# Two fused attention blocks in float32: the low part of phi on the two halves of the TensorE rows

## What is computed

```python
# layer 0, per image: x is [128, 1024]
theta = W_theta @ x + b_theta            # [64, 1024]
phi   = W_phi   @ x + b_phi              # [64, 1024]
f     = softmax(theta.T @ phi / sqrt(64))   # [1024, 1024], over the keys
x     = x + W_fuse @ (x @ f.T) + b_fuse
# layer 1
h = group_norm(x, 32 groups) * gn_w + gn_b
q, k, v = q_w @ h + q_b, k_w @ h + k_b, v_w @ h + v_b    # [128, 1024] each
f = softmax(q.T @ k / sqrt(128))
x = x + p_w @ (v @ f.T) + p_b
```

## Time and profile before

| | |
|---|---|
| Median of three runs | 2052.92 us |
| Span of the profiled execution | 2050.9 us (its own device time isn't given; the median lies 2.0 us above the span) |
| TensorE busy | 2024.2 us, 99% |
| VectorE busy | 1635.8 us, 80% |
| ScalarE busy | 1504.8 us, 73% |
| GpSimd busy | 1301.5 us, 63% |
| Mean granted TensorE clock | 0.999 of 2.4 GHz |

### The profile page before, as it was taken

The page is one execution under the profiler, slowest core; times in us unless marked ns, Lnnn a source line. Parts: engine busy times, 40 slices in busy tenths (PEclk is TensorE's granted clock), DMA queues, the critical chain, the costliest instruction groups (busy, mean ns, idle before and its releaser), DMA issues.

```text
span 2050.9 us, 39045 instructions
## 1 busy us (share of the span) xinstructions
PE 2024.2 (99%) x11460; PEld 1724.3 (84%) x11460; DVE 1635.8 (80%) x2538; ACT 1504.8 (73%) x2696; POOL 1301.5 (63%) x1669
## 2 busy tenths in 40 slices
PE   7899999999999999999999999999999999999998
PEld 5788888888888888888888888888888888888886
DVE  6788788878888887888888887888888888878875
ACT  5777777777777777777777777777777777777764
POOL 4666656666666666666665666666666656666654
PEclk9999999999999999999999999999999999999999
DMA  2111111111111011111111111111111111111100
GB/s 62 52 36 48 41 41 41 36 46 41 41 51 37 34 41 51 41 41 36 46 41 41 43 36 44 41 51 41 41 36 46 41 41 41 36 46 41 36 16 31
DMA packets 38326, 84.71 MB, mean 41 GB/s; under 512 B 4640, under 2 KB 5536, under 8 KB 38304
## 3 DMA queue, kind: packets, MB, share of 16 engines
q1 hardware_dynamic: 38304, 84.43, 13.2%
HBM read 34.08 MB, written 16.78 MB: 25 GB/s over the span
## 4 chain that ended last, share of the span: by engine, by line
PE 96%; DVE 0%; POOL 0%; issue 0%; ACT 0%; ACTq 0%; POOLq 0%
PE o_ps L317 35%; PE s_ps L317 28%; PE t_ps L331 21%; PE m_ps L317 6%; PE m_ps L425 3%; PE m_ps L427 1%; PE m_ps L409 0%; PE m_ps L405 0%; DVE et_lo L595 0%; DVE neg_max L605 0%; DVE y_sb L628 0%; ACT e L537 0%; POOL h_lo L718 0%; ACT et_hi L476 0%; POOL e L702 0%
## 5 line engine op out<-in xcount | busy, mean ns | idle before, releaser
L702 POOL TENSOR_SCALAR e<-e,rden 128x1024 f32<-128x1024 f32 x512 | 578.2, 1129 | 548.4 <-DVE rden L585 544.9
L476 ACT ACTIVATE et_hi<-t_ps 128x512 fp32r<-128x512 f32 x1024 | 557.5, 597 | 456.5 <-PE t_ps L331 455.3
L595 DVE TENSOR_TENSOR et_lo<-t_ps,et_hi 128x512 fp32r<-128x512 f32 x1024 | 659.9, 684 | 240.8 <-ACT et_hi L476 231.2
L605 DVE TENSOR_REDUCE neg_max<-s_ps 128x1 f32<-128x1024 f32 x512 | 622.0, 1215 | 2.2 <-PE s_ps L317 2.2
L537 ACT ACTIVATE e<-s_ps,neg_max 128x1024 f32<-128x1024 f32 x512 | 574.8, 1123 | 9.0 <-DVE neg_max L605 4.0
L331 PEld LDWEIGHTS t_ps<-ident_sb,e 128*128 128x128 f32 x4096 | 477.2, 140 | 75.0 <-POOL e L702 8.9
L331 PE MATMUL t_ps<-ident_sb,e 128*128 128x128 f32 x4096 | 531.7, 273 | 6.3 <-POOL e L702 5.5
L317 PE MATMUL o_ps<-et_hi,v_hi 128*128 128x512 f32 x1024 | 421.5, 412 | 2.1 <-DVE y_sb L628 1.9
L317 PE MATMUL o_ps<-et_lo,v_hi 128*128 128x512 f32 x1024 | 402.6, 393 | 0.0
L317 PE MATMUL o_ps<-et_hi,v_lo 128*128 128x512 f32 x1024 | 399.9, 391 | 0.0
L317 PE MATMUL s_ps<-phi,theta 128*128 128x512 f32 x1024 | 301.8, 417 | 1.3 <-ACT e L537 1.0
(11 more groups left out here) (95 smaller groups left out, 2193.1 us busy)
## 6 DMA issues: line engine op xcount, KB each, us to landing
xs<-in_x SPq DMA_DIRECT2D x32, 512.0 KB, 3.4
phi<-phi SPq DMA_DIRECT2D x64, 256.0 KB, 3.1
xr<-in_x SPq DMA_DIRECT2D x32, 512.0 KB, 3.3
x_res<-x SPq DMA_DIRECT2D x64, 256.0 KB, 2.3
out_y<-y_sb SPq DMA_DIRECT2D x64, 256.0 KB, 2.1
w_f<-in_w_fuse_t SPq DMA_DIRECT2D x1, 64.0 KB, 2.4
ident_sb<-in_ident SPq DMA_DIRECT2D x1, 64.0 KB, 2.1
p_t<-in_p_w_t SPq DMA_DIRECT2D x1, 64.0 KB, 2.2
```

What stands on the lines that cost most here:

```text
L476: nc.scalar.activation(et_hi[t // GROUP % 2][:, GROUP * half:GROUP * (half + 1), cols], t_ps[half][:, :].rearrange("k (b q) -> k b q", b=G ...
L595: nc.vector.tensor_tensor(et_lo[g][:, blocks, cols], t_ps[half][:, :].rearrange("k (b q) -> k b q", b=GROUP), et_hi[g][:, blocks, cols].bi ...
L605: nc.vector.tensor_reduce(neg_max[:, s % 4:s % 4 + 1], s_ps[:, s % 2, :], AX.X, ALU.max, negate=True).then_inc(s_max, 1)
L702: return nc.gpsimd.tensor_scalar(*args)
```

## The change

In layer 0 the products with phi's low part no longer take theta's low part along. Each uses 64 rows: the one for the first half of the keys takes theta's high part and phi's low part in rows 0:D, the one for the second half takes them in rows D:C. For this, theta's high part is needed in rows 64 to 127 as well, in a new buffer `theta_low`, which a further DMA fills behind the one of L303. So the term theta low x phi low is left out of the sum. The two full products come first, then the pair, which writes to the two different PSUM banks of the slot's scores.

```diff
+        theta_low = sb("theta_low", [C, N], F32R)
...
                     sp.wait_ge(s_direct, before(direct_at, i, s) + 1)
                     sp.dma_start(phi2[0:D, :, cols].bitcast(F32), phi2[D:C, :, cols].bitcast(F32)).then_inc(s_phi, 16)
+                    sp.dma_start(theta_low[D:C, cols].bitcast(F32), theta2[0:D, cols].bitcast(F32)).then_inc(s_phi, 16)
...
-                        pe.wait_ge(s_phi, 16 * before(tp_at, i, 0))
+                        pe.wait_ge(s_phi, 32 * before(tp_at, i, 0))
...
                 if s < PHASE:
-                    mm = product(out, [(theta2[:, qs], phi2[:, 0, ks]), (theta2[:, qs], phi2[:, 1, ks])])
+                    product(out, [(theta2[:, qs], phi2[:, 0, ks])], stop=False)
+                    if half == 1:
+
+                        first, last = slice(0, HALF), slice(HALF, N)
+                        product(s_ps[:, s % 2, first], [(theta2[0:D, qs], phi2[0:D, 1, first])], start=False)
+                        mm = product(s_ps[:, s % 2, last], [(theta_low[D:C, qs], phi2[D:C, 1, last])], start=False)
```

## The result

The changed kernel takes 2094.18 us (median of four runs, 2093.86 to 2095.19), the kernel before 2052.91: a ratio of 1.0201, with a 95% interval of 1.0186 to 1.0215. The forecast was 1997 us. It is 41.3 us slower than the kernel before, 0.161 us for each of the 256 slots of layer 0. The profiled execution has a span of 2092.6 us.

What follows compares the result with a forecast made beforehand. TensorE was taken to bound the kernel: 2052.9 us, less 59.5 for the pairs, plus 1 (GpSimd), 2.3 (images 0 and 1) and 0.6 (first DMA), gave 1997.3, said as 1997 us; range of all cases 1990 to 2085.

Steps and rivals of the forecast that it cites:

- What bounds the kernel: Whole kernel: TensorE, busy 99% of the span; time taken from its list leaves the kernel until another engine becomes late.
- What is removed: Layer-0 scores: with full overlap a slot pays for three products, not four, 0.2325 us in each of 256 slots, 59.5 us less.
- The price of the pair itself: Two 64-row products in a layer-0 slot: from 0.2325 us gained to a loss from emptying and exposed weight loads at two changes.
- the best case: Layer-0 pair: the second product starts with the first, loads hidden, 0.2325 us less a slot; full overlap given chance 0.37.
- the drain: Rival: TensorE empties at each change of rows, two a slot; 2072 us alone, 2123 or 2168 with loads; chance 0.31.
- the emptying: TensorE letting its array empty at a change between 128 and 64 rows: 0.154 us each, two a slot.
- break-even: Cost of one change of rows, two a layer-0 slot, from which the drain decides against the pair: 0.116 us.
- the emptying without a load: Drain alone at two changes a slot, no exposed load: +0.076 us a slot, 2072 us; half of the 0.31 chance.
- What is late next: Other engines' cover in slots 0 to 7: GpSimd's runs out in slot 6, adding 1 us; the DVE's holds.
- the place that the prediction named second: DVE's low part of k1 ahead of the unit reusing `m_ps`: 0.80 us of cover, two slots take 0.47, so it holds.
- The DMA: Further 128 KB transfer on SyncE's queue: hidden with 11 us of cover, except 0.6 us once before the first scores.

Runs made afterwards that it cites:

- the run with six full products: Kernel before with each product with phi's low part issued twice on all 128 rows, six products a layer-0 slot: 2163.30 us, ratio 1.0537.
- the grouped run: Changed kernel with low pairs of tiles 1 and 2, 3 and 4, 5 and 6 issued together at the ends of slots 1, 3, 5: 2069.88 us.

## Why the prediction was wrong

*What bounds the kernel* held: TensorE's list is the kernel's time before and after, and what lengthened a slot's list moved the time by nearly as much; the part that falls into the waits of the first images is lost (5.7 us in the run with six full products).

*What is removed* held in size. The pair runs as one product: 0.229 us for a further pair, 0.244 us more when the two are kept apart, against the 0.2325 assumed.

*The price of the pair itself* is the step that failed. I took the best case, which puts nothing in the sum for the change from 128 to 64 rows and back, and the reason was that all loads were hidden: "the first of the pair should find its weights there". But all those loads were of 128 rows under products of 128 rows; they say nothing on a change. A load of the other kind isn't brought in early. It is held until about 0.10 us past the columns of the running product and then is exposed for 0.11 us: about 0.20 us a change (0.203 with two, 0.19 with four), 0.40 us a slot against 0.23. The term that the sum lacks is 2 x 256 x 0.20 = 102 us: with it, 1997 us becomes 2099, against the 2094 measured.

The rival that came true, the drain, was sized in parts. What the prediction called the emptying, the time for which the load is held, is 0.10 us and not 0.154: the duration of a product beyond its pitch was the wrong measure of it. That it is the array emptying is a reading; the runs show the wait. The prediction's break-even, 0.116 us a change, would have decided with the emptying alone for a gain; what tips it is the load. The exposed load is 0.11 us, near the 0.10 us read from the value products behind a 128-column product, and far from its whole duration of 0.188 us. Both parts together gave 0.276 us a slot and 2123 us in the prediction; it was 0.161 us and 2094 us. The range ended at 2085, since it took in the emptying without a load, a case that none of these runs shows. The Trainium skill ("TensorEngine Tiling (Array Packing)", Key Properties) says that changing the tiling mode drains TensorE. The trace agrees, with the 0.10 us for which the next load is held.

"TensorE: Matmul & The Clock Gate" of the Trainium skill (Part 3) says that products in different row groups run together; the runs agree, with starts 0.00 to 0.01 us apart and one product's time for two.

*What is late next* wasn't put to the test, as the slots became longer: GpSimd's waits fell from 5.5 to 2.6 us. That small covers matter was seen elsewhere: in the grouped run 0.30 us of waiting came from VectorE's low part of k1, the place that the prediction named second.

*The DMA*: hidden but at the start, as predicted. The first scores start at 18.03 us against 17.10, 0.9 us later where 0.6 was said, and the DMA alone cost 0.9 us in its run (2053.91 against 2052.97).

## What to carry to other kernels

Two half-row products in the two halves of the rows do share one product's time, but each change between whole and half rows cost 0.2 us here, so a group of one pair (0.23 us gained, 0.40 us paid) loses. A group of two won a little: 0.04 us a slot where each slot had one (2152.91 against 2163.30 us), and 0.12 us in the chain where one stood at the end of slot 1, next to nothing where one stood in the middle of slot 5. Larger groups should win more, but none was set against its twin of full rows. Count the changes before counting the pairs, and look whether every neighbour in TensorE's list can have the same number of rows. And a load that is hidden in the trace is hidden only for the kinds of neighbours that the trace shows.

## What the runs showed that I had not expected

Products of 96 rows between products of 128 cost nearly nothing (0.3%), those of 64 rows 9.5%. The two weight loads of a pair start at the same time and take as long as one (0.18 us each). Transposes between score products cost the same 0.11 us each as eight in a row, for no load starts more than one product ahead. And three pairs cost what one pair and two full products do, 2095.31 against 2094.18 us.
